# SBUF placement at multiples of 1 KB and a new order of the three partial products in a Strassen-style MoE layer

## What is computed

```python
    xn = _layernorm(x, axis=-1)
    x = x + _L0_attn_ref(xn, ...) + _L0_ffn_ref(xn, ...)
    # in the expert branch:
    scores = jnp.einsum('BTC,CE->BTE', x, gate_w)
    probs = jax.nn.softmax(scores, axis=-1)
    top_p, top_idx = jax.lax.top_k(jnp.transpose(probs, (0, 2, 1)), cap)
    xin = jnp.take_along_axis(x[:, None, :, :], top_idx[..., None], axis=2)
    h = jax.nn.gelu(jnp.einsum('BElC,ECH->BElH', xin, w1), approximate=False)
    y = jnp.einsum('BElH,EHC->BElC', h, w2)
    out = out.at[b_idx, top_idx].add(y * top_p[..., None])
```

## The kernel before

| operand | role | even experts | odd experts |
|---|---|---|---|
| `w1h` blocks | stationary, 512 B | 512 and 0 | 128 and 640 |
| `w1l` blocks | stationary, 512 B | 512 and 0 | 672 and 160 |
| `xs_hi`, `xs_lo` | moving, 1 KB | 672 | 672 |
| `g_hi`, `g_lo` blocks | stationary, 512 B | 672 and 160 | 672 and 160 |
| `w2h` | moving, 1 KB | 128 | 672 |
| `w2l` | moving, 1 KB | 128 | m 0 to 3 at 672, m 4 to 7 at 576 |

## Time and profile before

### The profile page before, as it was taken

The page is one execution under the profiler, slowest core; times in us unless marked ns, Lnnn a source line. Parts: engine busy times, 40 slices in busy tenths (PEclk is TensorE's granted clock), DMA queues, the critical chain, the costliest instruction groups (busy, mean ns, idle before and its releaser), DMA issues.

```text
span 2338.6 us, 81411 instructions
## 1 busy us (share of the span) xinstructions
PE 2264.5 (97%) x34252; PEld 2095.6 (90%) x34252; DVE 1531.5 (65%) x3103; ACT 1391.5 (59%) x2553; POOL 1283.3 (55%) x2012
## 2 busy tenths in 40 slices
PE   6999999999999988999999999999999999999998
PEld 5777777777777778999999999999999999999998
DVE  3555555656666657996766767667667667676674
ACT  4555565555655546556666656666666666666664
POOL 4444444444544455655566666666566576575453
PEclk9999999999999999999999999999999999999999
DMA  3232222322223312232324324224234233232332
GB/s 120 74 95 85 75 76 83 94 84 76 76 75 94 98 61 71 49 77 50 50 44 89 46 46 91 43 49 86 47 52 82 47 54 80 48 54 43 51 50 33
DMA packets 129368, 157.72 MB, mean 67 GB/s; under 512 B 11008, under 2 KB 118656, under 8 KB 129024
## 3 DMA queue, kind: packets, MB, share of 16 engines
q0 software_dynamic: 49152, 67.14, 17.8%
q1 hardware_dynamic: 79872, 85.54, 11.6%
HBM read 85.53 MB, written 67.11 MB: 65 GB/s over the span
## 4 chain that ended last, share of the span: by engine, by line
PE 55%; DVE 0%; POOL 0%; issue 0%; ACT 0%; DVEq 0%
PE attn L1779 28%; PE scores L1698 18%; PE front L1698 7%; PE front L1688 2%; POOL out L798 0%; DVE rows L211 0%; DVE topi L207 0%; DVE top L202 0%; DVE hidden L1263 0%; DVE xs_lo L1233 0%; ACT res L949 0%; DVE rows L223 0%; PE scores L233 0%; PE scores L232 0%; DVE rows L225 0%
## 5 line engine op out<-in xcount | busy, mean ns | idle before, releaser
L1779 PE MATMUL attn<-w_hi,g_hi 128*128 128x256 f32 x2048 | 581.5, 284 | 2.5 <-DVE g_lo L1274 2.4
L1779 PE MATMUL attn<-w_lo,g_hi 128*128 128x256 f32 x2048 | 578.3, 282 | 0.0
L1779 PE MATMUL attn<-w_hi,g_lo 128*128 128x256 f32 x2048 | 578.1, 282 | 0.0
L987 ACT ACTIVATE hidden<-hidden 128x512 f32<-128x512 f32 x384 | 235.4, 629 | 263.9 <-DVE hidden L1263 263.9
L1779 PEld LDWEIGHTS attn<-w_hi,g_hi 128*128 128x128 f32 x2048 | 388.6, 190 | 3.0 <-DVE g_lo L1274 2.7
L1779 PEld LDWEIGHTS attn<-w_hi,g_lo 128*128 128x128 f32 x2048 | 388.3, 190 | 0.0
L1779 PEld LDWEIGHTS attn<-w_lo,g_hi 128*128 128x128 f32 x2048 | 388.0, 189 | 0.0
L1698 PE MATMUL scores<-xs_hi,w_hi 128*128 128x256 f32 x1280 | 362.0, 283 | 8.4 <-DVE xs_lo L1233 6.3
L1698 PE MATMUL scores<-xs_lo,w_hi 128*128 128x256 f32 x1280 | 362.8, 283 | 0.0
L1263 DVE TENSOR_TENSOR hidden<-front,hidden 128x512 f32<-128x512 f32 x256 | 176.3, 689 | 284.0 <-PE front L1698 270.7
L1698 PE MATMUL scores<-xs_hi,w_lo 128*128 128x256 f32 x1280 | 361.0, 282 | 0.0
(11 more groups left out here) (182 smaller groups left out, 5154.4 us busy)
## 6 DMA issues: line engine op xcount, KB each, us to landing
x<-in_x SPq DMA_DIRECT2D x32, 512.0 KB, 5.3
w_stage<-in_w SPq DMA_DIRECT2D x16, 1024.0 KB, 6.4
xn_rows<-xn SPq DMA_DIRECT2D x32, 512.0 KB, 3.2
res<-in_x SPq DMA_DIRECT2D x32, 512.0 KB, 3.8
out<-res SPq DMA_DIRECT2D x32, 512.0 KB, 3.4
xg<-xn_rows,step_idx POOLq DMA_INDIRECT x256
out<-y,scatter_idx POOLq DMA_INDIRECT x128, 3.9
out<-res,scatter_idx POOLq DMA_INDIRECT x128, 3.9
```

The costliest lines, as they stand in the source:

```text
L987: act.activation(own(q, p), src, ACT.Gelu).then_inc(g_ready, 1)
L1779: last = pe.matmul(yb[k % 2][:, 0:D], g_[:, m, cols], w, start=start and m == first and i == 0, stop=end, skip_group_check=True)
```

## The change

Two edits. First, placement: the small tensors are allocated first, and every large buffer, of the attention and of the expert stage, is placed with `at` at a multiple of 1024 bytes (with a few exceptions that follow directly on another tensor: `v_unbiased`, `state`, the second `v_parity`). In the expert stage every moving block then begins at 0 modulo 1024 and every stationary block at 0 or 512. Sizes, lifetimes and which buffer lies over which stay as they were in essence. Second, the order within the three partial products: `quarter` and `down` now issue high by high, then the low stationary part with the same moving operand, then the high stationary part with the low moving one. In the attention's products the order stays. No instruction, wait or semaphore is added or removed.

```diff
+        gst_w = sb("gate_stage", [P, DH, E])
+        st = sb("ln_stats", [P, TT, 6])
...
+        sidx = sb("scatter_idx", [P, GRP], U32)
         route = Routing(ctx, nc, cst)
...
+        KB = 1024
+        bv = at("bv_rows", [P, D], F32, 53 * KB)
+        w_hi = [None if i == 2 else at(f"w_hi{i}", [P, DH, D], F32R, o * KB)
+                for i, o in enumerate((54, 56, None, 58))]
+        w_lo = [at(f"w_lo{i}", [P, DH, D], F32R, (60 + 2 * i) * KB) for i in range(4)]
+        xb = [at(f"x{i}", [P, TT, D], F32, (68 + 4 * i) * KB) for i in range(2)]
+        xn = at("xn", [P, TT, D], F32, 76 * KB)
+        vg_hi = at("vg_hi", [P, DH, VG], F32R, 80 * KB)
...
+        x_hi = at("x_hi", [P, DH, S], F32R, 90 * KB)
+        x_lo = at("x_lo", [P, DH, S], F32R, 94 * KB)
...
+        a_hi = at("a_hi", [P, DH, S], F32R, 171 * KB)
+        a_lo = at("a_lo", [P, DH, S], F32R, 175 * KB)
...
-        LATE = 186880
-        w1h = [at("w1_hi0", [P, 7, QF], F32R, LATE), at("w1_hi1", [P, 7, QF], F32R, 56448)]
-        w1l = [at("w1_lo0", [P, 7, QF], F32R, LATE + K1), at("w1_lo1", [P, 7, QF], F32R, 167584)]
-        s2 = at("w2_stage", [P, FT, D], F32, LATE + 2 * K1)
-        w2h = [at("w2_hi0", [P, FT, D], F32R, 78976), at("w2_hi1", [P, FT, D], F32R, 106144)]
-        w2l = [[at(f"w2_lo{i}{j}", [P, FT // 2, D], F32R, o) for j, o in enumerate(os)]
-               for i, os in enumerate(((70784, 74880), (181920, LATE + 2 * K1 + K2 + 1088)))]
...
-        xs_hi = at("xs_hi", [P, 7, HALF], F32R, 87712)
-        xs_lo = at("xs_lo", [P, 7, HALF], F32R, 87712 + KX)
...
-        g_hi = at("g_hi", [P, FT, SL], F32R, 134816)
-        g_lo = at("g_lo", [P, FT, SL], F32R, 151200)
+        w1h = [at("w1_hi0", [P, 7, QF], F32R, 183 * KB), at("w1_hi1", [P, 7, QF], F32R, 57 * KB)]
+        w1l = [at("w1_lo0", [P, 7, QF], F32R, 197 * KB), at("w1_lo1", [P, 7, QF], F32R, 165 * KB)]
+        s2 = at("w2_stage", [P, FT, D], F32, 211 * KB)
+        w2h = [at("w2_hi0", [P, FT, D], F32R, 79 * KB), at("w2_hi1", [P, FT, D], F32R, 105 * KB)]
+        w2l = [[at(f"w2_lo{i}{j}", [P, FT // 2, D], F32R, o * KB) for j, o in enumerate(os)]
+               for i, os in enumerate(((71, 75), (179, 219)))]
...
+        xs_hi = at("xs_hi", [P, 7, HALF], F32R, 87 * KB)
+        xs_lo = at("xs_lo", [P, 7, HALF], F32R, 94 * KB)
...
+        g_hi = at("g_hi", [P, FT, SL], F32R, 133 * KB)
+        g_lo = at("g_lo", [P, FT, SL], F32R, 149 * KB)
...
-                    for i, (w_, x__) in enumerate(((w1h, xs_hi), (w1h, xs_lo), (w1l, xs_hi))):
+                    for i, (w_, x__) in enumerate(((w1h, xs_hi), (w1l, xs_hi), (w1h, xs_lo))):
...
-                    for i, (g_, w) in enumerate(((g_hi, hi), (g_hi, lo), (g_lo, hi))):
+                    for i, (g_, w) in enumerate(((g_hi, hi), (g_lo, hi), (g_hi, lo))):
```

More of the change, by code:

```diff
@@ L254, in layer @@
         vec = sb("vec", [P, V_N])
+        gst_w = sb("gate_stage", [P, DH, E])
+        st = sb("ln_stats", [P, TT, 6])
+        mv = sb("ln_mv", [P, TT, 2])
+        ln_ve, ln_r, ln_y, ln_a, ln_m = (sb(f"ln_{n}", [P, TT]) for n in ("ve", "r", "y", "a", "m"))
+        ost = sb("o_stats", [P, DH, 6])
+        gm = sb("g_moments", [P, DH, 2])
+        gs = sb("g_means", [P, DH, 2])
+        gn_ve, gn_r, gn_y, gn_a, gn_m, gn_s, gn_b = (sb(f"gn_{n}", [P, DH])
+                                                     for n in ("ve", "r", "y", "a", "m", "s", "b"))
+        idx = sb("step_idx", [P, GRP], U32)
+        sidx = sb("scatter_idx", [P, GRP], U32)
         route = Routing(ctx, nc, cst)
@@ L261, in layer @@
         wst = s1[:, 0:4, :].rearrange("p a (b n) -> p (a b) n", n=D).rearrange("p (i h) n -> p i h n", h=DH)
[L262 to L289, removed]
@@ L290, in layer @@
-        gn_ve, gn_r, gn_y, gn_a, gn_m, gn_s, gn_b = (sb(f"gn_{n}", [P, DH])
-                                                     for n in ("ve", "r", "y", "a", "m", "s", "b"))
+        KB = 1024
[4 more added lines that the diff above has]
+        xb = [at(f"x{i}", [P, TT, D], F32, (68 + 4 * i) * KB) for i in range(2)]
@@ new lines, in layer @@
+        xn = at("xn", [P, TT, D], F32, 76 * KB)
+        vg_hi = at("vg_hi", [P, DH, VG], F32R, 80 * KB)
+        vraw = at("v_unbiased", [P, TT, VG], F32, 80 * KB + DH * VG * 4)
+        tm = [at(f"state{i}", [P, NSUB - 1, DH, 2 * HD], F32, 90 * KB - (2 - i) * (NSUB - 1) * DH * 2 * HD * 4)
+              for i in range(2)]
+        x_hi = at("x_hi", [P, DH, S], F32R, 90 * KB)
+        x_lo = at("x_lo", [P, DH, S], F32R, 94 * KB)
+        q32 = at("q32", [P, DH, S], F32, 98 * KB)
+        qm = [at(f"q_parity{i}", [P, DH, 2, S], F32, (102 + 8 * i) * KB) for i in range(2)]
@@ new lines, in layer @@
+        qd = [at(f"q_decayed{i}", [P, DH, S], F32, (118 + 4 * i) * KB) for i in range(2)]
+        k32 = [at(f"k{i}", [P, DH, S], F32, (126 + 4 * i) * KB) for i in range(2)]
+        kn = at("k_natural", [P, TT, D], F32, 134 * KB)
+        vm = [at(f"v_parity{i}", [P, TT, VW], F32, 138 * KB + i * TT * VW * 4) for i in range(2)]
+        s_sb = [at(f"s_sb{i}", [P, PAIRS, 512], F32, (155 + 8 * i) * KB) for i in range(2)]
+        a_hi = at("a_hi", [P, DH, S], F32R, 171 * KB)
+        a_lo = at("a_lo", [P, DH, S], F32R, 175 * KB)
@@ L293, in layer @@
+        o32 = at("o32", [P, DH, S], F32, 179 * KB)
         tb = ctx.enter_context(nc.psum_tensor("front", [P, DH, 512], F32))
@@ L382, in layer @@
         HALF = SL // 2
-        K1 = 7 * QF * 4
-        K2 = FT * D * 4
-        KX = 7 * HALF * 4
-        LATE = 186880
-        w1h = [at("w1_hi0", [P, 7, QF], F32R, LATE), at("w1_hi1", [P, 7, QF], F32R, 56448)]
-        w1l = [at("w1_lo0", [P, 7, QF], F32R, LATE + K1), at("w1_lo1", [P, 7, QF], F32R, 167584)]
-        s2 = at("w2_stage", [P, FT, D], F32, LATE + 2 * K1)
-        w2h = [at("w2_hi0", [P, FT, D], F32R, 78976), at("w2_hi1", [P, FT, D], F32R, 106144)]
-        w2l = [[at(f"w2_lo{i}{j}", [P, FT // 2, D], F32R, o) for j, o in enumerate(os)]
-               for i, os in enumerate(((70784, 74880), (181920, LATE + 2 * K1 + K2 + 1088)))]
@@ L393, in layer @@
-        xg = [at(f"xg{k}", [P, D], F32, 53248 + 1024 * k if k < 3 else LATE + 2 * K1 + K2) for k in range(GRP)]
-        idx = at("step_idx", [P, GRP], U32, LATE + 2 * K1 + K2 + 1024)
-        sidx = at("scatter_idx", [P, GRP], U32, LATE + 2 * K1 + K2 + 1056)
-        xs_hi = at("xs_hi", [P, 7, HALF], F32R, 87712)
-        xs_lo = at("xs_lo", [P, 7, HALF], F32R, 87712 + KX)
-        xsum = at("x_sums", [P, 4, HALF], F32, 87712 + 2 * KX)
-        hid = {q: at(f"hidden{q}", [P, 2, 2, HALF], F32, o)
-               for q, o in (("22", 114336), ("21", 118432), ("11", 122528), ("12", 130720))}
@@ L401, in layer @@
-        y = [at("y", [P, GRP, D], F32, 126624), res]
-        g_hi = at("g_hi", [P, FT, SL], F32R, 134816)
-        g_lo = at("g_lo", [P, FT, SL], F32R, 151200)
+        w1h = [at("w1_hi0", [P, 7, QF], F32R, 183 * KB), at("w1_hi1", [P, 7, QF], F32R, 57 * KB)]
+        w1l = [at("w1_lo0", [P, 7, QF], F32R, 197 * KB), at("w1_lo1", [P, 7, QF], F32R, 165 * KB)]
+        s2 = at("w2_stage", [P, FT, D], F32, 211 * KB)
+        w2h = [at("w2_hi0", [P, FT, D], F32R, 79 * KB), at("w2_hi1", [P, FT, D], F32R, 105 * KB)]
@@ new lines, in layer @@
+        w2l = [[at(f"w2_lo{i}{j}", [P, FT // 2, D], F32R, o * KB) for j, o in enumerate(os)]
+               for i, os in enumerate(((71, 75), (179, 219)))]
+        xg = [at(f"xg{k}", [P, D], F32, (53 + k) * KB) for k in range(GRP)]
+        xs_hi = at("xs_hi", [P, 7, HALF], F32R, 87 * KB)
+        xs_lo = at("xs_lo", [P, 7, HALF], F32R, 94 * KB)
+        xsum = at("x_sums", [P, 4, HALF], F32, 101 * KB)
+        hid = {q: at(f"hidden{q}", [P, 2, 2, HALF], F32, o * KB)
+               for q, o in (("22", 113), ("21", 117), ("11", 121), ("12", 129))}
@@ L405, in layer @@
+        y = [at("y", [P, GRP, D], F32, 125 * KB), res]
+        g_hi = at("g_hi", [P, FT, SL], F32R, 133 * KB)
+        g_lo = at("g_lo", [P, FT, SL], F32R, 149 * KB)
         xb_ = {p: sbk[:, i, :] for i, p in enumerate("AB")}
```

## The result

The changed kernel takes 2347.86 us, median of 7 runs (2343.98 to 2355.72), against 2335.57 us of before in the same comparison. The ratio is 1.0048 with a 95% interval of 1.0032 to 1.0065: slower by 0.5%, where 2320 us were forecast. That is the time of the prediction's first rival, the conflict of equal offsets (2347 us, chance 0.27).

The account below looks back on a forecast made before the run. PE's matmul spacing was taken to bound the kernel. Even steps gain 5.6 and odd 10.4 us, other parts zero: 2335.57 - 16.0 = 2319.6, say 2320 us; range 2300 to 2349 us.

Parts of the forecast that it names:

- first rival: Expert stage and attention: PE's stationary and moving reads disturb each other most at offsets equal modulo 512; 2347 us, chance 0.27.
- The bound: Expert steps: PE never rests, so matmul spacing sets their length; other engines have some 7 us of cover.
- Addresses do act on PE.: Expert steps: even and odd differ only in weight addresses, 22.15 against 22.30 us, some 0.9 ns of 118 per matmul.
- I take 117.1 ns: Expert matmuls after the change: spacing taken from the even experts' w1 matmuls, whose stationary blocks lie at 0 or 512.
- `down` rows: Half 2 of `down`: 118.75 ns where operand offsets differ, 119.6 ns where both are at 672 or 160.
- the odd w1 set: Odd experts' w1 weights at 128, 640, 672, 160: 119.2 ns, as slow with a high half not equal to the moving offset.
- The `value_gate` rows: Attention: moving operands on or near 1 KB run at 0.455 to 0.464 ns a column, so alignment gains and costs nothing.
- The sum: Expert steps become 0.87 + 180 x 0.1171 = 21.95 us; 28 even and 29 odd steps save 16.0 us.
- The excess grows with the columns: Matmul spacing over 109 ns: 16 ns at 512 columns and 9 at 256; held against the much faster rival, chance 0.09.
- the 512-column matmuls should stay at 234 ns: Attention projections: spacing unchanged by the placement, counted as zero with bounds of plus and minus 2 us.
- The order: New order of partial products in `quarter` and `down`: zero effect, bound 3.4 us either way.
- Even and odd steps should in any case become nearly equal: Expert stage: both weight sets get the same offsets modulo 1024; if steps stay unequal, address bits above 1 KB matter.

Follow-up runs that it names:

- the streams: Kernels with the whole computation left out: PE alone runs loops of identical matmuls at chosen operand offsets; 113.3 to 120.0 ns per matmul at 256 columns.
- place_only: The changed kernel with the old order of the three partial products put back; 2342.59 us, ratio to before 1.0040.
- all_up_256: The changed kernel with every stationary and moving operand of the expert stage placed 256 bytes higher; 2340.72 us, ratio to before 1.0031.

## Why the prediction was wrong

**The bound.** Right. PE's spacing sets the steps, before and after; the other engines' 15.4, 14.2 and 15.1 us are still covered, and in the steps PE waits for nothing, before or after.

**"Addresses do act on PE."** Right, and it was the argument on which everything rested. The Trainium skill, "TensorE: Matmul & The Clock Gate", section "Step-by-step: what each phase is for", has the two read ports of PE independent, and "SBUF — State Buffer", section "Who interferes with whom", says "PE and ACT never wait on anyone." By these taken together the offsets would be worth nothing, and the runs do not agree: with nothing but PE at work, the offset between the two operands moved a matmul from 113.3 to 120.0 ns. That the two reads of PE collide is my explanation; what is shown is the dependence on the difference.

**The step that failed: "I take 117.1 ns, because it is the row whose stationary operands lie just as all of them will."** The row's stationary offsets were those of the change, but its moving operands were at 672, so the difference was 96, and the change made it 0: the matmul took 120.0 ns where the sum had 117.1, and the step 22.46 us where it had 21.95. I took the offset of one operand for the variable, though I had written down the other reading as a rival, with the `down` rows as its evidence (0 at 119.6, 32 at 118.75 ns). The listed expert rows fit the difference: where it was 0, they were slow. The weight against it, that the odd w1 set was slow "with a high half that is not equal", was a row of both halves together; the low half is one in three of its matmuls, and its difference was 0.

**The `value_gate` rows.** They were read as a moving operand on 1 KB that gains nothing and costs nothing (the two rows lie four matmuls apart and not three; the 1056 columns are right). Their differences were 160 (672 or 160 minus 0 or 1024) and, for `vg_hi`'s second block at 64 bytes after one, 96. They said nothing about a difference of 0.

**The sum.** By the rival's own working the step was to be 22.40 us and was 22.46, as the spacing was 120.0 and not 119.6: in the worst stretch of the earlier trace rows the first two of the 24 matmuls came after 113 and 119 ns, and all later ones at 120. 28 x 0.31 + 29 x 0.15 = 13 us, where the trace has 13.5 over 56 steps. That the rival's 2347 us met the measured 2347.86 so closely is partly luck: it had the steps 3 us too short, and it charged 1.8 us to the attention's 512-column matmuls, which became faster.

**"The excess grows with the columns" and "the 512-column matmuls should stay at 234 ns."** Neither holds as a rule. 512 columns went from 234 to 229.5 ns on average for the `x` projections and to 226.9 for the output projection, counted from the starts in both traces; the first row below is a start of L1381 in the changed kernel, the second three matmuls later, 0.68 us, where the earlier trace rows have 0.234 for each, 0.70 for three.

```profile
622.06 0.39 PE L1381 MATMUL front<-a_hi,w_hi 128*128 128x512 f32 x1
...
622.74 0.39 PE L1381 MATMUL front<-a_hi,w_hi 128*128 128x512 f32 x1
```

That is close to the streams' 234.3 at 96 and 226.7 at 0. The excess over the columns at 2.4 GHz was 21 ns at 512 and some 10.5 at 256 columns before, both at a difference of 96, where it does grow; at 0, where the change put them all, it is 13.3 ns for both. The two rows had been right for their own difference only. For the 1152 matmuls of 512 columns this gives some 6 us, and PE was indeed busy for 808.8 us up to 860 us, where before it was 814.8, with the same 21674 matmuls; but the first expert step begins no earlier in the profiled execution. Starts of that step in the ten profiled executions of full kernels lie between 887.1 and 900.2 us, so a gain of some us in the attention can't be shown from single profiles. The medians lean towards it: `place_only` and `all_up_256` have the steps of the changed kernel and so its 13.5 us, but their medians lie only 10.2 and 8.3 us above that of before, 2332.43 us on their chip. How much of the gain reached the end stays open.

**The order.** Zero was right for the changed placement (`place_only` has the same steps). At the placement of before, the odd steps gained 0.10 us, 29 x 0.10 = 3 us, within the bound of 3.4 us given for it.

**The check written into the prediction.** "Even and odd steps should in any case become nearly equal": they did, to 0.01 us, and that is what the low bits of the addresses being the only variable looks like. **The range**, 2300 to 2349 us, holds the measured time only because it took in the rival; the sign of the forecast was wrong.

## What to carry to other kernels

Where PE never rests and a step is nothing but matmuls, the placement of its operands is a variable worth a per cent or two, and the one to look at is the stationary block's offset minus the moving block's, modulo 256 bytes. Round addresses for everything make that difference 0, here the slowest value for 256 moving columns of fp32r (160 is as slow) and the fastest for 512; a stream of a few dozen matmuls with nothing else running gives the value for one's own shape in a few microseconds, but where it has two rates, only the whole kernel tells which it gets. When two variants of one step differ in the trace, write out every variable in which they differ, relations between operands too, before taking a row's value over.

## What the runs showed that I had not expected

- One steady loop of identical matmuls has two steady rates at some differences, 113.3 and 117.8 ns at 64, and keeps either for 180 matmuls, with equal clock and equal instructions; in the kernels' steps bound by PE it changed only at a block of eight 128-column transposes, and not at every one.
- At a difference of 0, each matmul costs 13.3 ns over its columns at 2.4 GHz, whether it has 256, 320, 384 or 512 of them; 128 and 192 columns both cost 111.7 ns, so at 192 columns and below something other than the moving stream sets the spacing.
- For fp32r with a weight load for each matmul, keeping the stationary or the moving block gave nothing: 120.0 ns in all cases at a difference of 0 or 256.
